# Experts' up projection in three fp32r passes, normalising on ScalarE, shared buffers in a GNN and mixture-of-experts layer

## The chip, the core and the metric

One core of a Trainium2 chip runs the whole layer. The metric is the time of one launch in microseconds of the device; lower is better. The engines that matter here are TensorE (PE for matmuls, PEld for loading the stationary operand), VectorE (DVE), ScalarE (ACT), GpSimd (POOL), and the queue of SyncE (SP), which starts most of the transfers.

## What is computed

The reference is a graph attention layer over 4096 nodes of 512 values, a dense feed-forward net, and then a mixture of experts. The change lies in the last part only:

```python
def _L0_ffn_ref(x, router_w, w1, b1, w2, b2, gamma, beta):   # x: 4096 rows of 512, 8 experts, 256 hidden
    logits = xf @ router_w
    gate_vals, idx = jax.lax.top_k(logits, 2)
    gates = jax.nn.softmax(gate_vals, axis=-1)
    for e in range(E):
        h = jax.nn.relu(xf @ w1[e] + b1[e]) @ w2[e] + b2[e]
        y = _layernorm(xf + h, gamma[e], beta[e])
        w = jnp.sum(jnp.where(idx == e, gates, 0.0), axis=-1)
        out = out + w[:, None] * y
    return out
x = x + _L0_ffn_ref(_layernorm(x, axis=-1)[None], ...)[0]
```

All of it is float32. The kernel computes each row only for the two experts that the router picks.

## The kernel before

The program is a row of blocks with a barrier between them: sorting the edges and the projections of q, k, v, attention, output projection with feed-forward net, and `experts`, which runs alone from about 2945 us to the end. In it every engine has its own instruction stream, and the streams are ordered by semaphores. A `Ring` counts the tiles of a buffer: `ring.wait(eng, i, u)` waits until tile u of turn i is done.

`experts` has four stages.

The router stage takes the 32 tiles of 128 rows of z3 in four turns of eight, each in two halves. PE transposes a tile (L2094), ACT copies it to `z_cols` (L1912), and after four tiles PE multiplies with the router weights (L2107). DVE copies the result (L1969), PE turns it back (L2116), DVE keeps the logits (L1971). SP loads the rows ahead, and behind them, in one queue, b1, w1, w2, b2, gamma, beta and the first rows of x3 (L1794 to L1800).

The list stage is a chain on DVE with some matmuls: top two experts, the place of each row in a list sorted by expert, and which expert each slot of 128 rows has (`expert_of`). It ends with `row_of` (L2042), which sets `s_ready`. Every engine then waits for `s_ready` and for the weights (`s_w`).

The loop takes 72 slots in nine turns of eight (`TURN`). For slot u: POOL gathers the rows by an indirect DMA (L1844) and adds b2 to them (L1852, `res`); PE transposes them (L2094); ACT copies the columns to `zT` (`columns`, L1922); PE multiplies with w1 (`up`, L2150); ACT copies the result (`hidden`, L1927), PE transposes it (L2157), ACT applies bias and Relu (`hidden_columns`, L1934); PE multiplies with w2 (`down`, L2165). DVE adds `res` (L2051, into `y`), takes mean and variance (L2053, L2055), ACT the square root (L1951), DVE the reciprocal (L2057) and normalises (L2058). POOL multiplies by gamma (L1869), DVE adds beta (`shift`, L2064), SP stores the tile.

The order of each engine's stream is written out by hand. PE, in step u: rows of u+2, up of u+1, down of u, hidden of u+1 turned. ACT: `columns(u+2)`, `hidden(u+1)`, `hidden_columns(u+1)`, square root of u. DVE: `norm(u)`, `shift(u-1)`; the last step of a turn has `shift(7)` behind it. POOL: gather of u+4, residual of u+1, gamma of u. `zT`, `up_ps`, `down_ps`, `res` have two buffers, `y` four. `expert(eng, i, u)` reads the number of the slot's expert into a register of the engine, ahead of each operation that uses that expert's weights.

The sum stage gathers for each node its two results (L1897), DVE adds them, times the gates, to x3 (L2080, L2082), and SP stores.

An fp32 matmul stands in the trace as two records of each call.

## Time and profile before

| what | us |
|---|---|
| median of 3 runs | 3532.98 |
| fastest and slowest of them | 3523.99 and 3536.39 |
| the profiled execution's own time | 3529.53 |
| its span, first to last instruction | 3527.8 |
| mean granted TensorE clock | 0.902 of full |

Busy over the whole span: PE 80%, DVE 71%, POOL 62%, PEld 51%, ACT 42%. These are averages over stages with different limits, so the profile has to be read by stage. A timeline line has the start in us, the duration in us, the engine, the line and the operands, and in brackets the idle time of the engine before it and what ended that.

### The profile page before, as it was taken

The numbers are of one execution on the slowest core, as the hardware profiler recorded it, in microseconds if no ns is written. First come the engines' busy times: TensorE is split into PE (matmuls) and PEld (weight loads), VectorE is DVE, ScalarE is ACT, GpSimd is POOL, SyncE is SP. The second block draws the span as 40 slices with busy tenths as digits, with TensorE's granted clock in tenths as the row PEclk, the third lists the DMA queues.
The fourth block names the chain that finished last, engine by engine and source line by source line (L and its number), as shares of the span: only waits on it lengthen the run. The fifth ranks groups of instructions, "written<-read, shape, count | busy, mean of one in ns | idle before, by whom it ended". The sixth has DMA issues, their size and how long they took to land. (4 is left out here: it accounts for less than half of the span.)

```text
span 3527.8 us, 57760 instructions
## 1 busy us (share of the span) xinstructions
PE 2810.0 (80%) x12074; PEld 1806.6 (51%) x12075; DVE 2507.1 (71%) x5087; ACT 1472.7 (42%) x4642; POOL 2197.7 (62%) x2242
## 2 busy tenths in 40 slices
PE   7888888853878888886888888884999997699950
PEld 5555555531333333334665555553888884466630
DVE  6766666634989999999888888885555551577764
ACT  6322222212655655565554544542344442144420
POOL 2477777776777777776777777771222220188866
PEclk9788888876999999998999999996999998799985
DMA  3444444444777777776777777776222223533349
GB/s 104 175 153 157 138 151 159 138 158 124 210 208 210 209 208 206 210 209 187 213 213 213 211 212 213 213 213 212 85 86 86 86 70 119 201 110 113 113 127 314
DMA packets 234986, 594.26 MB, mean 168 GB/s; under 512 B 51889, under 2 KB 60978, under 8 KB 229938
## 3 DMA queue, kind: packets, MB, share of 16 engines
q0 software_dynamic: 127104, 362.93, 36.3%
q1 hardware_dynamic: 103666, 222.27, 17.7%
q10 hardware_dynamic: 4032, 7.34, 0.6%
q14 instruction: 158, 1.29, 0.1%
q8 instruction: 26, 0.43, 0.1%
HBM read 500.22 MB, written 92.15 MB: 168 GB/s over the span
## 5 line engine op out<-in xcount | busy, mean ns | idle before, releaser
L1214 PE MATMUL at_bank<-product,v_hot 128*128 128x260 f32 x2432 | 629.3, 403 | 119.9 <-DVE product L970 110.6
L1168 PE MATMUL at_bank<-wide,hot_t 128*128 x1216 | 611.8, 625 | 127.8 <-ACT hot_t L1036 66.8
L803 POOL DMA_INDIRECT fetched<-t_k,at_index x608 | 583.0, 959 | 192.8 <-issue 134.1
L812 POOL DMA_INDIRECT fetched<-t_v,at_index x608 | 579.1, 953 | 195.2 <-issue 132.3
L348 POOL DMA_INDIRECT records<-staged,address x544 | 533.3, 980 | 265.0 <-issue 164.9
L1214 PEld LDWEIGHTS at_bank<-product,v_hot 128*128 128x128 f32 x2432 | 442.5, 195 | 301.2 <-issue 126.8
L886 DVE TENSOR_TENSOR product<-at_bank,fetched 128x512 f32<-128x512 f32 x608 | 412.6, 680 | 53.0 <-issue 37.1
L970 DVE TENSOR_TENSOR product<-fetched,at_turn 128x520 f32<-128x520 f32 x608 | 404.4, 686 | 61.8 <-DMA fetched<-t_v,at_index 30.1
L1168 PEld LDWEIGHTS at_bank<-wide,hot_t 128*128 128x128 f32 x1216 | 205.4, 193 | 381.7 <-issue 336.1
L617 PE MATMUL qkv_prod<-wide 128*128 128x512 f32 x768 | 378.2, 653 | 0.0
L843 DVE TENSOR_REDUCE raw_score<-product 128x7 f32<-128x448 f32 x608 | 347.1, 573 | 0.0
L1044 ACT ACTIVATE product<-product 128x64 f32<-128x64 f32 x912 | 228.1, 250 | 282.2 <-DVE product L886 281.2
L1109 ACT ACTIVATE v_hot<-at_shared 128x128 f32<-128x128 f32 x608 | 188.1, 309 | 363.2 <-PE at_bank L1214 362.8
L961 DVE TENSOR_TENSOR wide<-at_bank,wide 128x260 f32 x608 | 230.8, 420 | 61.8 <-issue 29.1
L617 PEld LDWEIGHTS qkv_prod<-wide 128*128 128x128 f32 x768 | 158.9, 211 | 193.4 <-issue 193.4
L1396 POOL TENSOR_TENSOR f_base<-f_x 128x512 f32<-128x512 f32 x32 | 41.3, 1291 | 331.0 <-DVE f_x L1445 328.9
L1078 ACT ACTIVATE at_shared<-iota_f,low_neg 128x128 f32<-128x128 f32 x608 | 234.9, 386 | 2.4 <-ACT v_hot L1109 2.1
L598 PE MATMUL ranks<-counts,low_hot_t 128*128 (+1 forms) x1088 | 178.4, 337 | 66.6 <-issue 53.2
L598 PEld LDWEIGHTS ranks<-counts,low_hot_t 128*128 128x128 f32 x1088 | 175.6, 257 | 71.9 <-issue 71.7
L1573 PE MATMUL f_up<-f_zT,f_w 128*128 128x256 f32 x1536 | 189.8, 284 | 0.0
L1573 PE MATMUL f_down<-f_w,f_hT 128*128 128x512 f32 x768 | 185.6, 397 | 2.3 <-issue 2.3
L1573 PEld LDWEIGHTS f_up<-f_zT,f_w 128*128 128x128 f32 x1536 | 185.1, 190 | 2.1 <-ACT f_h L1530 1.3
(294 smaller groups left out, 4253.8 us busy)
## 6 DMA issues: line engine op xcount, KB each, us to landing
row_bc<-in_src SPq DMA_DIRECT2D x34, 1024.0 KB, 4.7
by_slot<-m_y SPq DMA_DIRECT2D x72, 256.0 KB, 2.0
low_bc<-low_row SPq DMA_DIRECT2D x34, 512.0 KB, 5.5
fetched<-t_k,at_index POOLq DMA_INDIRECT x608, 3.7
fetched<-t_v,at_index POOLq DMA_INDIRECT x608, 3.8
records<-staged,address POOLq DMA_INDIRECT x544, 2.1
t_v<-wide SPq DMA_DIRECT2D x32, 260.0 KB
wide<-in_x SPq DMA_DIRECT2D x32, 256.0 KB, 2.9
```

What stands on the lines that cost most here:

```text
L348: eng.indirect_dma_start(records, bass.IndirectOffsetOnAxis(address[:, b, u:u + 1], 0), staged[:, b, u, :], None,).then_inc(put[b][u], 16)
L598: nc.tensor.matmul(ranks[b % 2][:, u * BLOCKS:(u + 1) * BLOCKS], low_hot_t[:, b % 2, u * P:(u + 1) * P], counts[:, :, bass.ds(i * 2 * B + ...
L617: last = nc.tensor.matmul(prod[n][:, :], zT[:, c, kc * P:(kc + 1) * P], w[:, n, kc, :], start=(kc == 0), stop=(kc == KC - 1))
L803: eng.indirect_dma_start(fetched[:, n % SLOTS, 0:C], None, k, bass.IndirectOffsetOnAxis(index[:, t:t + 1], 0)).then_inc(s_row[n % SLOTS], 16)
L812: eng.indirect_dma_start(fetched[:, n % SLOTS, :], None, v, bass.IndirectOffsetOnAxis(index[:, t:t + 1], 0)).then_inc(s_row[n % SLOTS], 16)
L843: nc.vector.tensor_reduce(raw[:, b, u % PAIR, u // PAIR, 0:heads], product[:, u % 4, 0:heads * D].rearrange("p (h d) -> p h d", d=D), AX.X ...
L886: nc.vector.tensor_tensor(product[:, u % 4, 0:C], q_edge[u % 4][:, :], fetched[:, u % SLOTS, 0:C], ALU.mult).then_inc(r_product.sem(u), 1)
L970: nc.vector.tensor_tensor(product[:, u % 4, :].rearrange("p (h w) -> p h w", h=HEADS), fetched[:, u % SLOTS, :].rearrange("p (h w) -> p h ...
L1078: nc.scalar.activation(away[:, u % 4, :], iota_f[:, :], ACT.Abs, bias=low_neg[:, bass.ds(back_of(m) * TURN + u, 1)]).then_inc(r_v_away.sem ...
L1168: nc.tensor.matmul(q_edge[u % 4][:, :], hot_t[:, g % 2, u % BATCH * P:(u % BATCH + 1) * P], q_sb[:, bass.ds(at, 1), :].rearrange("p a c -> ...
L1214: last = nc.tensor.matmul(bank[g % 2 * 2 + n][:, 0:HALF], hot[:, u % 4, :], product[:, u % 4, n * HALF:(n + 1) * HALF], start=first, stop= ...
L1573: last = nc.tensor.matmul(out, stationary(a, k), moving(b, k), start=(k == 0 and n == 0), stop=(k == chunks - 1 and n == len(PASSES) - 1))
```

## The change

1. `up` multiplies in fp32r. w1 and the columns are split into a large part (rounded to fp32r) and a small part (what is left), and three products are summed: large by large, large by small, small by large. Each 128x256 product is one record instead of two, and there are 12 records for a slot instead of 8.
2. The large part of the columns is ACT's copy, the small part a new subtraction on DVE, `small_columns(u+2)`, ahead of `norm(u)`; the first two stand ahead of the loop.
3. w1 is no longer loaded by SP. ACT's queue loads one expert at a time (512 KB) in the router stage, ACT rounds it (`large_w1`, ahead of the second tile of each half), DVE subtracts (ahead of its copy of the router's result).
4. DVE no longer normalises. It computes `offset` = -mean / root (one column), and ACT applies scale and offset in one Identity activation behind the square root.
5. `y`, `res`, `h_sb`, `hT` lie in the memory of `z_cols`; raw w1 and, at the end, `acc` lie in that of two experts' w2; the list stage's one-hot buffers lie in `zT` and `rows_sb`. So SP waits with w2 for the last small part of w1, and loads the first rows of x3 only after the last `down`.

```diff
-        w1_sb, w2_sb = sb("w1", [P, E, KC, F]), sb("w2", [P, E, FC, C])
+        w1_sb = sb("w1", [P, 2, E, KC, F], F32R)
+        w2_sb = sb("w2", [P, E, FC, C])
...
-        zT = sb("zT", [P, 2, C])
-        z_cols = sb("z_cols", [P, 2, KC, HALF * P])
+        zT = sb("zT", [P, 2, 2, C], F32R)
+        early = sb("early", [P, 2 * KC * HALF * P])
...
+        z_cols = early[:, :].rearrange("p (b k r) -> p b k r", b=2, k=KC)
...
+        y, res, h_sb, hT = reused(0, 4, C), reused(4 * C, 2, C), reused(6 * C, 2, F), reused(7 * C, 2, FC, P)
+        acc = w2_sb[:, 0:2, :, :].rearrange("p e f c -> p (e f) c")
+        raw = w2_sb[:, 0:2, :, :].rearrange("p e f c -> p e (f c)")
...
-            eng.dma_start(w1_sb[:, :, :, :], w1.rearrange("e (k p) f -> p e k f", p=P)).then_inc(s_w, 16)
+            r_w1_small.wait(eng, T // TURN - 1, 1)
             eng.dma_start(w2_sb[:, :, :, :], w2.rearrange("e (k p) c -> p e k c", p=P)).then_inc(s_w, 16)
...
             by_turn(eng, TURNS, store)
+            e_down.wait(eng, TURNS - 1, TURN - 1)
+            for u in range(HALF):
+                eng.dma_start(acc[:, u, :], x3[u * P:(u + 1) * P, :]).then_inc(c_x3.sem(u), 16)
...
         @block.scalar
...
+            def load_w1(i, half):
+                r_w1_small.wait(eng, i, half - 2)
+                eng.dma_start(raw[:, half, :].rearrange("p (k f) -> p k f", k=KC),
+                              w1[bass.ds(i * 2 + half, 1), :, :].rearrange("a (k p) f -> p (a k) f", p=P)
+                              ).then_inc(r_w1_raw[half], 16)
+
+            def large_w1(i, half):
+                eng.wait_ge(r_w1_raw[half], i * 16 + 16)
+                nc.scalar.copy(flat(w1_sb[:, 0, bass.ds(i * 2 + half, 1), :, :].rearrange("p a k f -> p a (k f)")),
+                               raw[:, half, :]).then_inc(r_w1_large.sem(half), 1)
+
+            load_w1(0, 0)
+            load_w1(0, 1)
...
+                    if m == 1:
+                        large_w1(i, half)
                     r_turn.wait(eng, i, u)
...
+                    if more and m == HALF - 1:
+                        load_w1(i + 1, half)
...
                     e_var.wait(eng, i, u)
-                    nc.scalar.activation(root[:, :], mean_var[:, 1:2], ACT.Sqrt, bias=eps[:, :]).then_inc(e_root.sem(u), 1)
+                    nc.scalar.activation(spread[:, :], mean_var[:, 1:2], ACT.Sqrt, bias=eps[:, :]).then_inc(e_root.sem(u), 1)
+                    e_offset.wait(eng, i, u)
+                    nc.scalar.activation(y[:, u % 4, :], y[:, u % 4, :], ACT.Identity, bias=offset[:, :], scale=root[:, :]
+                                         ).then_inc(e_norm.sem(u), 1)
...
         @block.vector
...
+                    r_w1_large.wait(eng, i, half)
+                    of = bass.ds(i * 2 + half, 1)
+                    nc.vector.tensor_tensor(flat(w1_sb[:, 1, of, :, :].rearrange("p a k f -> p a (k f)")), raw[:, half, :],
+                                            flat(w1_sb[:, 0, of, :, :].rearrange("p a k f -> p a (k f)")), ALU.subtract
+                                            ).then_inc(r_w1_small.sem(half), 1)
...
                 e_root.wait(eng, i, u)
-                per.link(nc.vector.reciprocal(root[:, :], root[:, :]))
-                nc.vector.tensor_scalar(mine, mine, mean_var[:, 0:1], root[:, :], ALU.subtract, ALU.mult
-                                        ).then_inc(e_norm.sem(u), 1)
+                e_norm.wait(eng, i, u - 1)
+                per.link(nc.vector.reciprocal(root[:, :], spread[:, :]))
+                nc.vector.scalar_tensor_tensor(offset[:, :], mean_var[:, 0:1], -1.0, root[:, :], ALU.mult, ALU.mult
+                                               ).then_inc(e_offset.sem(u), 1)
+
+            def small_columns(i, u):
+                e_zT.wait(eng, i, u)
+                e_up.wait(eng, i, u - 2)
+                nc.vector.tensor_tensor(zT[:, 1, u % 2, :], turned[u % 2][:, :], zT[:, 0, u % 2, :], ALU.subtract
+                                        ).then_inc(e_zT_small.sem(u), 1)
...
+            def body(i, more):
                 for u in range(TURN):
+                    if u < TURN - 2 or more:
+                        small_columns(i, u + 2)
                     norm(i, u)
                     if u:
                         shift(i, u - 1)
                 shift(i, TURN - 1)
...
             def up(i, u, e):
                 e_zT.wait(eng, i, u)
+                e_zT_small.wait(eng, i, u)
                 for kc in range(KC):
-                    last = nc.tensor.matmul(up_ps[u % 2][:, :], zT[:, u % 2, kc * P:(kc + 1) * P], flat(w1_sb[:, e, kc, :]),
-                                            start=(kc == 0), stop=(kc == KC - 1))
+                    for a, b in ((0, 0), (0, 1), (1, 0)):
+                        last = nc.tensor.matmul(up_ps[u % 2][:, :], zT[:, a, u % 2, kc * P:(kc + 1) * P],
+                                                flat(w1_sb[:, b, e, kc, :]), start=(kc == 0 and a == b),
+                                                stop=(kc == KC - 1 and a == 1))
```

## Rows read from the trace of the kernel before

**Rows 1.** Busy time by stretch: stretch, length, each engine's busy (records), clock, DMA, GB/s
```profile
core 0: us, PE busy (x) PEld busy (x) DVE busy (x) ACT busy (x) POOL busy (x), PEclk, DMA share, GB/s
2945.00:3016.00 71.00, 55.24 (x221) 22.95 (x221) 6.77 (x15) 18.77 (x33) 1.45 (x9) 0.86 0.63 202
...
3025.00:3039.00 14.00, 1.92 (x8) 1.78 (x8) 12.52 (x33) 0.00 (x0) 0.00 (x0) 0.50 0.99 416
...
3081.00:3400.00 319.00, 299.15 (x1224) 196.88 (x1223) 244.45 (x408) 135.88 (x354) 261.42 (x220) 1.00 0.34 110
```

**Rows 2.** Timeline: the first and the last residual add of the 72
```profile
3076.00 0.69 DVE L2051 TENSOR_TENSOR m_y<-m_down,m_res 128x512 f32<-128x512 f32 x1 [16.94 <-PE m_down L2165]
...
3409.38 0.68 DVE L2051 TENSOR_TENSOR m_y<-m_down,m_res 128x512 f32<-128x512 f32 x1
```

**Rows 3.** Timeline of one slot: DVE and the square root
```profile
3216.71 0.69 DVE L2051 TENSOR_TENSOR m_y<-m_down,m_res 128x512 f32<-128x512 f32 x1 [0.75 <-PE m_down L2165]
...
3218.50 0.29 ACT L1951 ACTIVATE m_root<-m_mv,m_eps 128x1 f32<-128x1 f32 x1 [0.85 <-DVE m_mv L2055]
...
3219.03 0.81 DVE L2058 TENSOR_SCALAR m_y<-m_y,m_mv,m_root 128x512 f32<-128x512 f32 x1
...
3219.89 0.69 DVE L2064 TENSOR_TENSOR m_y<-m_y,m_beta 128x512 f32<-128x512 f32 x1
```

**Rows 4.** Timeline of another slot: DVE and POOL from normalising to the next add
```profile
3181.65 0.55 DVE L2058 TENSOR_SCALAR m_y<-m_y,m_mv,m_root 128x512 f32<-128x512 f32 x1
...
3182.37 1.27 POOL L1869 TENSOR_TENSOR m_y<-m_y,m_gamma 128x512 f32<-128x512 f32 x1 [0.79 <-DVE m_y L2058]
3182.51 1.67 DVE L2064 TENSOR_TENSOR m_y<-m_y,m_beta 128x512 f32<-128x512 f32 x1 [0.32 <-issue]
...
3184.11 0.68 DVE L2051 TENSOR_TENSOR m_y<-m_down,m_res 128x512 f32<-128x512 f32 x1
```

**Rows 5.** Chain that ended last, ahead of the loop: start us, us, what
```profile
3015.85 22.79 DMA m_beta<-in_L_ffn_beta
```

**Rows 6.** Timeline: the last operation of the list stage
```profile
3058.83 0.23 DVE L2042 CAST m_row_of<-m_down 128x72 int32<-128x72 f32 x1 [2.50 <-PE m_down L2139]
```

**Rows 7.** Groups by line, 3100 to 3400 us: count, busy us, mean ns, idle before
```profile
L2150 PE MATMUL m_up<-m_w,m_zT 128*128 x516 | 127.6, 390 | 11.8 <-issue 10.3
...
L1951 ACT ACT_TABLE_LOAD x7 | 9.0, 1283 | 0.1
```

**Rows 8.** Groups by line in the feed-forward stage, 2500 to 2930 us
```profile
L1573 PE MATMUL f_up<-f_zT,f_w 128*128 128x256 f32 x1392 | 170.4, 282 | 0.0
...
L1409 DVE TENSOR_TENSOR f_zT<-f_turned,f_zT 128x512 fp32r<-128x512 f32 x28 | 18.0, 686 | 38.0 <-ACT f_zT L1538 38.0
```

**Rows 9.** Groups by line, ACT, whole span: a 128x512 activation with constants
```profile
L1036 ACT ACTIVATE hot_t<-hot_t 128x512 f32<-128x512 f32 x152 | 93.2, 613 | 0.0
```

**Rows 10.** Groups by line, 2395 to 2470 us: weights split into large and small
```profile
L1409 DVE TENSOR_TENSOR f_w<-f_raw,f_w 128x1024 fp32r<-128x1024 f32 x4 | 4.9, 1225 | 2.6 <-ACT f_w L1511 2.4
L1508 ACT ACTIVATE f_w<-f_raw,f_gain 128x1024 fp32r<-128x1024 f32 x4 | 4.6, 1153 | 1.2 <-DMA f_raw<-in_L_gnn_W 0.9
...
L1511 ACT CAST f_w<-f_raw 128x1024 fp32r<-128x1024 f32 x4 | 4.2, 1044 | 2.8 <-DMA f_raw<-in_L_gnn_W 2.8
```

**Rows 11.** Timeline of half a turn of the router stage: last copies, router matmuls
```profile
2969.97 1.07 ACT L1912 COPY m_z_cols<-m_turned 128x512 f32<-128x512 f32 x2 [0.26 <-PE m_turned L2094]
...
2971.17 3.59 PE L2107 MATMUL m_down<-m_z_cols,m_router 128*8 128x512 f32 x8 [0.75 <-ACT m_z_cols L1912]
```

**Rows 12.** Timeline: the first sum of the last stage
```profile
3423.66 0.75 DVE L2080 SCALAR_TENSOR_TENSOR m_acc<-m_rows,m_gate,m_acc 128x512 f32<-128x512 f32 x1 [8.85 <-DMA m_rows<-by_slot,m_index]
```

**Rows 13.** Busy time by stretch: of the sort, of attention, of the feed-forward stage
```profile
224.00:251.00 27.00, 22.01 (x110) 14.99 (x110) 15.01 (x43) 5.39 (x8) 20.60 (x22) 0.81 0.49 172
988.00:1067.00 79.00, 63.01 (x188) 25.43 (x188) 71.80 (x137) 46.31 (x221) 60.10 (x63) 0.96 0.72 207
...
2477.00:2954.00 477.00, 464.29 (x2811) 408.23 (x2809) 237.32 (x490) 189.62 (x397) 118.50 (x97) 0.99 0.25 86
```

49 lines of the change are left out of this document (27 added, 22 removed).

## The prediction, written before the change was run

> **What bounds the kernel now.** I first read the busy times by stage [rows 1]. The diff touches only the last block, the mixture of experts: the router stage (2945 to 3016 us), the list stage (to 3058), the loop over the 72 slots, and the weighted sum. In the loop the reader is to see TensorE busy 299 of 319 us, DVE 244, POOL 261 and ACT only 136, at full clock. It looks like a matmul bound, but TensorE is no lone bottleneck. From the first residual add to the last there are 333.4 us for 71 steps [rows 2], 4.70 us a slot, so TensorE works 4.4 and idles 0.3 of each.
>
> Next the timeline of one slot on DVE [rows 3]. From the residual add (L2051, 3216.71) the chain runs through the batch-norm pair to the square root on ACT (3218.50), back to the reciprocal and to the normalising op L2058 (3219.03): 2.32 us. Every step waits for the one before, whatever TensorE does. Then come L2058, L2064 (adding beta to the slot before), and the next add. In the other timeline [rows 4] L2058 takes 0.55, L2064 begins 0.32 after its end, in the same moment in which POOL multiplies by gamma, and takes 1.67 instead of 0.68, and the next add starts at 3184.11. So a slot whose chain DVE carries alone lasts about 2.32 + 0.86 + 1.60 = 4.78 us. That serial path is as long as TensorE's, and the prediction turns on what becomes of it.
>
> For the other stages: the last weight transfer, issued at 3015.85, lands 22.79 later, at 3038.6 [rows 5], while the list is done only at 3058.83 [rows 6]. The weights have 20 us to spare.
>
> **The change part by part.**
>
> *Up projection, TensorE.* Now 1.98 us a slot (127.6 us over 64.5 slots) [rows 7]. The stage before runs the same three-pass form, 128x256, at 170.4 us for 1392 records, 0.122 each [rows 8]; 12 of them are 1.47 us. TensorE gains 0.51 us a slot, down to 3.9. It is worth 36 us only if nothing else holds the slot.
>
> *Small half of the columns, DVE.* One subtraction PSUM minus SBUF, 128x512 to fp32r: 0.686 in the FFN stage [rows 8]. It is put ahead of the residual add and needs the columns that ACT copies.
>
> *Normalising moves to ACT.* DVE drops L2058 (1.085 mean, 0.55 alone) and gets a one-column op, about 0.17 as the reciprocal has in such a chain; ACT gets a 128x512 Identity with scale and bias per partition. Bounds: 0.61 with constants [rows 9]; a per-partition operand adds 1.153 - 1.044 = 0.11 on 1024 columns [rows 10], so two make 0.83. I take 0.8; it can't cost nothing, as it stands between two waits.
>
> *The new DVE path.* Residual add to the offset op: 2.32 as before. What follows is the expert's register load, then L2064. In one slot [rows 4] L2064 starts 0.86 after the start of L2058, while in the other [rows 3] L2058 took longer (0.81) and L2064 followed at once, so the 0.86 counts from the issue of the op before it, and shortening that op doesn't shorten it. Then L2064 0.70, the small columns 0.70, the next add: 2.32 + 0.86 + 0.70 + 0.70 = 4.58 us.
>
> *The new path over ACT.* The columns copy for slot u+2 is behind the Identity of slot u-1 on ACT. Before, it started right behind the 0.29 square root and nobody on DVE wanted it. Now: 2.32, offset op to ACT 0.21, Identity 0.75 (back-to-back ACT ops overlap a little), columns 0.59, hand-over 0.04, small columns 0.70 = 4.61. Two rings of the same length, both above TensorE's 3.9 and POOL's 3.84 (261.4/319 of 4.70). The slot becomes 4.6, not 4.2.
>
> *Port.* L2064 and POOL's gamma collide now. After, L2064 starts 0.86 behind the offset op; gamma can start at 0.21 + 0.8 + 0.18 = 1.19 (0.18 is POOL's delay behind L2058's end [rows 4]). DVE is first, and L2064 stays at 0.70.
>
> *End of each turn of eight.* After slot 7 DVE does beta for slots 6 and 7 before the next small columns; slot 7's has to wait for gamma: 2.32 + 1.19 + 1.50 + 0.05 + 0.70 + 0.70 = 6.46. The table load of ACT at the head of a turn (1.28) [rows 7] ends at 0.21 + 0.8 + 0.17 + 1.28 + 0.59 = 3.05 after the offset op, under the 3.44 of that path, so it is hidden; the second lies in ACT's idle time. Step 0 to 1 has no beta and takes the ACT ring.
>
> *Loop.* 8 x 6.46 + 9 x 4.61 + 52 x 4.6 + 2 x 3.9 (the last two have no small columns) = 51.7 + 41.5 + 239.2 + 7.8 = 340.2 against 333.4: +6.8. Bounds: 4.48 a slot (Identity at 0.61, the DVE path overlapping the register load), 0 to -2; 4.75 (waits not fully hidden), +16.
>
> *Router stage.* ACT rounds one expert's w1 to fp32r (128x1024, 1.044 [rows 10]) ahead of the second columns copy of each half turn, eight times. In the half turn shown the last copies start at 2969.97 and the router matmuls wait for them until 2971.17, 0.75 idle [rows 11]. TensorE's fourth transposition waits for the second copy, and the copies are back to back in pairs, so the cast pushes the second, third and fourth copy back by its length: 8 x 1.04 = +8.3. DVE's subtraction (1.225 [rows 10]) lies under the 3.59 us of matmuls [rows 11]. The eight 512 KB loads are issued behind the fourth copy and have a half turn and more to land; the first two share the start with 2 MB of rows, +1.
>
> *Weights, SP queue.* Loading w2 waits for the last w1 subtraction, because raw w1 lies in w2's space: issue near 3018 instead of 2997, behind it b2, gamma, beta. But 4 MB are gone from the queue; 10 MB at the 416 GB/s seen [rows 1] need 25 us, done near 3045. The list ends near 3068. Hidden, 20 us spare; 0. Moving w1 off the queue gains nothing for the same reason.
>
> *x3 rows.* Loaded only after the last down projection, SP's queue behind the last store. The first sum waits 8.85 us for gathers anyway and starts at 3423.66 [rows 12], some 9 us after the last store is issued; 1 MB lands in less. 0 to +2, I take 0. The shared buffers y, h, hT and the lists have no wait that the order of the stages doesn't already meet.
>
> *Clock.* Here rows speak against the change. With TensorE 97% busy (FFN) the granted clock is 0.99; with 81% busy in the sort stage it is 0.81, with 80% in attention 0.96 [rows 13], and the experts' loop at 94% has 1.00 [rows 1]. The new loop has 3.9/4.75 = 82%. At half clock (1.2 of 2.4 GHz) TensorE needs 7.8 us a slot against 4.6, so each microsecond at half clock costs 0.4. Attention's 0.96 means 8% of the time: 340 x 0.08 x 0.4 = +11; the sort stage's 0.81 means 38%, +52; none is 0. I take a third of attention's share, +4, since no row tells how the chip weighs this mix, and the idle pieces here are spread evenly. The Trainium skill, "TensorE: Matmul & The Clock Gate", section "HAM oscillation", ties a fall to long idle gaps; by it there would be none here and the sum 4 us less. Whether the falls of the other stages came behind such gaps isn't shown by these rows.
>
> *Sum.* 6.8 + 8.3 + 1 + 4 = +20 on the profiled execution's 3529.5 us (span 3527.8): 3549.5. The median, 3533.0, is 3.5 above that execution, and runs scatter by 12 us, so I set 3551.
>
> **The rivals.**
>
> R1, the matmul gain comes through. It would if DVE's register load isn't counted from the issue and ACT takes the Identity in a gap, POOL being less disturbed. 4.70 - 0.51 = 4.19 a slot gives 71 x 4.19 + 8 x 1.8 = 312, -21, with router +9: 3521 (3508 to 3524). For it: DVE and POOL get rid of a contended op; steps as short as 4.1 occur now. Against: the two rings.
>
> R2, the clock falls as in the sort stage: +15 +52 at the worst, half of that likelier: 3575 to 3600.
>
> R3, the port goes to POOL. If the Identity ended before L2064 starts (under 0.47 us, or beta late by 0.3), L2064 would last 1.67 in every slot, as it does in one now [rows 4]: 71 x 0.98 = +70, 3620. That is the point from which it decides.
>
> R4, Identity isn't in the table of the square root: two loads of 1.28 in every slot, 72 x 2.56 = +184, 3735. Copy and Relu, however, run in all eight slots of a turn with one load before the square root (7 loads in 64 slots [rows 7]). The Trainium skill ("ScalarE: Activation LUTs", "Table sets") puts identity with relu and copy in every set; then there is no load, and the sum stays.
>
> R5, the clock holds and the router casts find idle time of ACT: 3551 - 4 - 8 = 3539.
>
> **How the numbers follow.** Forecast (3540 to 3564) 0.55, R5 0.05, R1 0.20, R2 0.12, R3 0.06, R4 0.02. The range 3512 to 3592 leaves out R3, R4, the lowest quarter of R1 and the highest third of R2, about 0.17. The likeliest case's own range is 3540 to 3564. 0.3% is 10.6 us, about what a measurement of this kernel can tell from no change, so the bounds are 3522.4 and 3543.6. Faster: three quarters of R1 and a little of the scatter, 0.17. Same: the rest of R1, R5 and 0.15 of the forecast, 0.25. Slower: the rest, 0.58.
>
> **What would show it.** L2150's group 1.47 us a slot; residual add to residual add 4.6 in the middle of a turn and over 6 at its boundary; TensorE busy about 82% of the loop; beta at 0.68 and no longer 1.67; ACT's Identity 0.75 to 0.83; the router stage 8 to 10 us longer; the time from last weights to list end still positive; granted clock under 1.00 in the loop. Wrong it would be if the step fell under 4.4 (then beta follows the offset op at once, or the columns copy runs ahead of the Identity), or if the loop shows half clock for over 30 us.

## The result, and the profile after

| | before | after |
|---|---|---|
| median, us (runs) | 3533.34 (4) | 3562.77 (4) |
| fastest and slowest | 3523.99 and 3536.39 | 3560.29 and 3563.92 |
| span of the profiled execution | 3527.8 | 3562.2 |
| mean granted TensorE clock | 0.902 | 0.902 |

The ratio is 1.0089, with a 95% interval of 1.0075 to 1.0103: the changed kernel is slower, by 0.9%. The profiled executions of columns_first and act_best_small (below) were among the slower runs of their kernels, so what is read from them rests as well on identity_late and best_three, whose profiles were not. The span grew by 34.4 us. It splits at four operations of the timeline, the counterparts of [rows 2, 6, 12]:

```profile
3067.92 0.23 DVE L2083 CAST m_row_of<-m_down 128x72 int32<-128x72 f32 x1 [2.50 <-PE m_down L2193]
...
3084.71 0.69 DVE L2092 TENSOR_TENSOR m_early<-m_down,m_early 128x512 f32<-128x512 f32 x1 [1.24 <-PE m_down L2222]
...
3442.62 0.68 DVE L2092 TENSOR_TENSOR m_early<-m_down,m_early 128x512 f32<-128x512 f32 x1
...
3457.05 0.75 DVE L2134 SCALAR_TENSOR_TENSOR m_w<-m_rows,m_gate,m_w 128x512 f32<-128x512 f32 x1 [8.70 <-DMA m_rows<-by_slot,m_index]
```

The list is done 9.1 us later than before (3067.92 against 3058.83), of which 2.4 lie ahead of the block. From there to the first residual add it takes 0.4 less than before. The loop, first to last residual add, takes 357.9 us against 333.4: +24.5. Last add to first sum is 14.43 against 14.28, the rest 105.1 against 104.1. So seven tenths of the loss are in the loop.

Busy time by stretch, most of the loop after, to be held against the third row of [rows 1]:

```profile
3085.00:3427.00 342.00, 291.00 (x1480) 186.50 (x1478) 238.94 (x470) 186.87 (x419) 239.37 (x216) 1.00 0.31 101
```

TensorE fell from 94% to 85% busy, VectorE from 77% to 70%, POOL from 82% to 70%, and ScalarE rose to 55%. No engine is near full, yet most slots got longer: the limit is a path, not an engine. The groups by line of the loop, 3090 to 3432 us, name its links (count, then busy us, mean ns of one, and the idle time ahead with what ended it):

```profile
L2206 PE MATMUL m_up<-m_w,m_zT 128*128 x809 | 116.2, 292 | 18.7 <-issue 17.2 <-DVE m_zT L2106 1.4
...
L1864 POOL TENSOR_TENSOR m_early<-m_rows,m_b 128x512 f32<-128x512 f32 x68 | 87.7, 1290 | 1.1
L1881 POOL TENSOR_TENSOR m_early<-m_early,m_gamma 128x512 f32<-128x512 f32 x67 | 85.8, 1280 | 76.6 <-ACT m_early L1986 76.6
...
L1986 ACT ACTIVATE m_early<-m_early,m_offset,m_root 128x512 f32<-128x512 f32 x67 | 54.5, 814 | 56.1 <-DVE m_offset L2100 56.1
...
L2106 DVE TENSOR_TENSOR m_zT<-m_turned,m_zT 128x512 fp32r<-128x512 f32 x67 | 46.3, 692 | 30.0 <-ACT m_zT L1955 29.5 <-issue 0.3
...
L2112 DVE TENSOR_TENSOR m_early<-m_early,m_beta 128x512 f32<-128x512 f32 x67 | 46.3, 691 | 30.4 <-issue 18.9 <-POOL m_early L1881 11.3
...
L2100 DVE SCALAR_TENSOR_TENSOR m_offset<-m_mv,m_root 128x1 f32<-128x1 f32 x67 | 37.4, 558 | 2.6 <-DVE m_root L2099 0.3
```

The up projection fell to 0.144 us a record (116.2 over 809), 1.72 for the twelve of a slot. ScalarE's Identity lasts 0.81. VectorE's offset operation, one column, lasts 0.56 in the mean. POOL, which used to be the busiest helper, now waits 76.6 us for the Identity.

The timeline of one slot and a half shows why (some VectorE, ScalarE and POOL rows from it; the residual add of VectorE is L2092, that of POOL L1864):

```profile
3195.25 1.28 POOL L1881 TENSOR_TENSOR m_early<-m_early,m_gamma 128x512 f32<-128x512 f32 x1 [1.05 <-ACT m_early L1986]
...
3196.67 0.99 POOL L1856 DMA_INDIRECT m_rows<-t_z,m_index  x1
...
3197.67 1.29 POOL L1864 TENSOR_TENSOR m_early<-m_rows,m_b 128x512 f32<-128x512 f32 x1
...
3198.49 0.50 DVE L2100 SCALAR_TENSOR_TENSOR m_offset<-m_mv,m_root 128x1 f32<-128x1 f32 x1
3199.03 0.82 ACT L1986 ACTIVATE m_early<-m_early,m_offset,m_root 128x512 f32<-128x512 f32 x1 [0.77 <-DVE m_offset L2100]
3199.36 0.69 DVE L2112 TENSOR_TENSOR m_early<-m_early,m_beta 128x512 f32<-128x512 f32 x1 [0.36 <-issue]
3199.75 0.56 ACT L1955 CAST m_zT<-m_turned 128x512 fp32r<-128x512 f32 x1
3200.02 1.27 POOL L1881 TENSOR_TENSOR m_early<-m_early,m_gamma 128x512 f32<-128x512 f32 x1 [1.06 <-ACT m_early L1986]
...
3200.34 0.69 DVE L2106 TENSOR_TENSOR m_zT<-m_turned,m_zT 128x512 fp32r<-128x512 f32 x1 [0.30 <-ACT m_zT L1955]
```

Read it along POOL. Its residual add runs from 3197.67 to 3198.96. The offset operation, issued at 3198.49, ends at 3198.99, 0.03 behind the end of POOL's residual add, where 0.16 is its length alone. So it is in all 57 slots in which it lasts over 0.2 us: it ends 0.02 to 0.04 behind that end. Identity follows at 3199.03, gamma at 3200.02 behind it, and then POOL's own queue: gather, and the next residual add. Gamma to gamma is 4.77, and every link is there: residual 1.29, 0.03 to the end of the offset operation, 0.04, Identity 0.82, 0.17, gamma 1.27, 0.15, gather 0.98, 0.02. It is a ring that passes from POOL to VectorE, from there to ScalarE and back to POOL, and TensorE isn't in it.

Twice in a turn POOL copies the next gather indices (L1847). In the middle of a turn it waits 0.91 with the gather behind the copy. The residual add then starts later, and the offset operation waits through all of it:

```profile
3227.74 1.01 POOL L1856 DMA_INDIRECT m_rows<-t_z,m_index  x1 [0.91 <-PE m_turned L2148]
...
3228.67 1.40 DVE L2100 SCALAR_TENSOR_TENSOR m_offset<-m_mv,m_root 128x1 f32<-128x1 f32 x1
3228.76 1.28 POOL L1864 TENSOR_TENSOR m_early<-m_rows,m_b 128x512 f32<-128x512 f32 x1
```

The steps between residual adds in a turn are 6.58 (slot 7 to 0), 4.63, 4.68, 4.77, 4.77, 5.67, 4.78, 4.76: 40.6 us against 37.6 before.

### The profile page after: what moved, and what is told of

Same layout as the page of the kernel before. It is cut to its first block and busy times, and to the rows that moved or that the text cites. A ratio compares the mean times of both kernels' runs of the same rounds, so it can differ in the third digit from the quotient of the medians.

```text
span 3562.2 us, 59000 instructions
## 1 busy us (share of the span) xinstructions
PE 2801.9 (79%) x12362; PEld 1794.8 (50%) x12363; DVE 2510.5 (70%) x5167; ACT 1535.3 (43%) x4722; POOL 2181.2 (61%) x2242
## 5 line engine op out<-in xcount | busy, mean ns | idle before, releaser
L1169 PEld LDWEIGHTS at_bank<-wide,hot_t 128*128 128x128 f32 x1216 | 206.4, 194 | 381.4 <-issue 333.4
L384 ACT ACTIVATE qkv_root<-qkv_mv,qkv_eps 128x1 f32<-128x1 f32 x64 | 18.9, 295 | 395.9 <-DVE qkv_mv L96 395.9
```

Source lines behind the costliest of these rows:

```text
L1169: nc.tensor.matmul(q_edge[u % 4][:, :], hot_t[:, g % 2, u % BATCH * P:(u % BATCH + 1) * P], q_sb[:, bass.ds(at, 1), :].rearrange("p a c -> ...
```

## The experiments

The kernels of group 1 in the table share a chip on which the kernel before took 3533.61 (7 runs). Those of groups 2 and 3 ran on another chip, where the kernel before took 18 to 21% longer (before: 4259.66 and 4163.65), and where the stages ahead of the block, whose code is the same in all, ended anywhere between 3718 and 3826 us (first residual add). Their intervals are up to 1.2% wide to either side, so ratios of those two groups can't decide differences of 1%. I read their loops instead, first to last residual add: their operations have the same durations as on the first chip (offset 0.16 alone, Identity 0.81, residual 1.28, gamma 1.27, gather 0.99), though no profile of the kernel before or of the changed one was taken there, so their loops are held against those of the first chip. The loops also differ in how often TensorE's granted clock fell to half; where that matters it is said.

| kernel | group | loop, us | median, us | ratio to before |
|---|---|---|---|---|
| before | - | 333.4 | 3533.34 | 1 |
| changed | - | 357.9 | 3562.77 | 1.0089 |
| one_pass | 1 | 358.7 | 3564.05 | 1.009 (1.0072 to 1.0108) |
| res_short | 1 | 342.6 | 3548.95 | 1.0048 (1.0031 to 1.0065) |
| cast_late | 1 | 359.2 | 3558.54 | 1.0076 (1.0059 to 1.0093) |
| act_norm | 1 | 355.4 | 3554.0 | 1.0054 (1.0035 to 1.0074) |
| dve_norm | 2 | 344.1 | 4295.57 | 1.0168 (1.0091 to 1.0244) |
| identity_late | 2 | 363.6 | 4292.93 | - |
| loads_early | 2 | 328.2 | 4251.89 | 1.0052 (1.0002 to 1.0103) |
| best_three | 2 | 480.4 | 4426.73 | 1.0461 (1.0376 to 1.0545) |
| columns_first | 3 | 357.7 | 4203.4 | 1.0034 (0.9974 to 1.0094) |
| act_best | 3 | 349.8 | 4222.6 | 1.0103 (0.9987 to 1.0219) |
| act_best_small | 3 | 480.3 | 4315.07 | 1.0385 (1.0326 to 1.0444) |
| dve_cast | 3 | 344.2 | 4232.6 | 1.0191 (1.0132 to 1.0251) |

**one_pass: is TensorE in the path?**

```diff
-                    for a, b in ((0, 0), (0, 1), (1, 0)):
+                    for a, b in ((0, 0),):
```

The kernel leaves out the two products with a small part.

> The changed kernel with one product (large by large) instead of three in the up projection; the two products with a small part are left out, so its output is less exact. All other work stays, the small columns on DVE too. Theory A (the ring DVE, square root, offset op, Identity, columns, small columns sets the slot at 4.77 us, and TensorE waits in it): TensorE loses 8 records, about 0.98 us a slot, and the step from residual add to residual add stays 4.77; the time stays within 5 us of the changed kernel. Rival B (TensorE, or the clock that follows it, still sets the slot): 72 x 0.98 = about 70 us less, or, if the clock falls because TensorE is less busy, longer by 10 us and more.

The loop took 358.7. A turn's steps are 6.80, 4.64, 4.67, 4.76, 4.76, 5.66, 5.20 and 4.43. The expectation named a fall of the clock as the other outcome, and there were falls: the granted clock was 0.91 over the loop, with TensorE 75% busy, and at half during part of two steps in each turn, those of 6.80 and 5.20. The steps at full clock decide: 4.64 to 4.76 and 5.66, within 0.02 of the changed kernel's, with eight of twelve up-projection records gone. In these TensorE isn't in the path. The step of 5.20 and the one of 4.43 behind it together take 0.1 more than the changed kernel's two, the boundary 0.2 more; what they would be at full clock isn't shown.

**res_short: does POOL hold the offset operation?**

```diff
-                eng.tensor_tensor(res[:, u % 2, :], rows_sb[:, u % TURN, :], flat(b2_sb[:, e, :]),
+                eng.tensor_tensor(res[:, u % 2, 0:1], rows_sb[:, u % TURN, 0:1], flat(b2_sb[:, e, 0:1]),
```

POOL adds one column; the other 511 of the residual are left out.

> The changed kernel with POOL's residual add (rows plus b2) cut from 512 columns to one; the other 511 columns of the residual are left out. Theory A1 (the offset op on DVE, 0.16 alone, waits up to 0.35, and once a turn 1.25 us, until POOL's residual add lets go of a path to SBUF that both use): the offset op takes 0.16 in every slot, the step falls from 4.77 to 4.4 to 4.5 and the one of 5.67 disappears; a turn goes from 40.65 to about 38.5, the loop is 18 to 20 us shorter. Rival A2 (the op itself costs 0.5 in this place, whatever POOL does): nothing changes in the loop, under 3 us. Rival C (POOL's own chain of gather, residual and gamma sets the slot): it loses 1.3 us a slot and the loop 50 us or more.

Loop 342.6, -15.3, where 18 to 20 were expected. Offset operation and what follows in one slot:

```profile
3196.31 0.68 DVE L2092 TENSOR_TENSOR m_early<-m_down,m_early 128x512 f32<-128x512 f32 x1
...
3198.61 0.16 DVE L2100 SCALAR_TENSOR_TENSOR m_offset<-m_mv,m_root 128x1 f32<-128x1 f32 x1
3198.81 0.81 ACT L1986 ACTIVATE m_early<-m_early,m_offset,m_root 128x512 f32<-128x512 f32 x1 [0.43 <-DVE m_offset L2100]
3199.47 0.69 DVE L2112 TENSOR_TENSOR m_early<-m_early,m_beta 128x512 f32<-128x512 f32 x1 [0.70 <-issue]
```

It lasts 0.16 in all 72 slots, and 42 of the 71 steps are 4.42 to 4.44. 4.42 is the ring over ScalarE that the prediction had at 4.61: 2.30 to the offset operation, 0.20, then, start to start, 0.72 (Identity), 0.59 (columns), 0.61 (small columns). The step with the index copy stayed at 5.3, which I had expected to fall further, and three of the boundary steps, with half clock in them, took 7.1 to 7.2 instead of 6.5. A reservation: a short residual add also takes 1.1 us out of POOL's ring, so this run alone doesn't separate holding the offset operation from POOL's queue being long. In the timeline they are one ring.

**cast_late: what do the casts cost in the router stage?**

```diff
-                    if m == 1:
-                        large_w1(i, half)
...
-                    if more and m == HALF - 1:
-                        load_w1(i + 1, half)
+                    if m == HALF - 1:
+                        large_w1(i, half)
+                        if more:
+                            load_w1(i + 1, half)
```

> The changed kernel with ACT's rounding of w1 behind the fourth columns copy of each half turn instead of ahead of the second, so that it runs beside the router matmuls. If the cast in the copies' path costs what was forecast (1.04 us, eight times), the router stage is 8 us shorter and nothing else moves. Rival: the weights, now rounded and loaded later, delay the next rounding or w2, and the stage or the start of the loop is as late as before or later; then 0 or positive.

The first residual add came at 3077.67 instead of 3084.71, 7.0 us earlier. Of these 1.2 lie ahead of the block, where the kernels don't differ; from the block's start to the end of the list cast_late takes 5.9 less, so the casts cost 5.9 here and not 8.3. The same move gives 6.5 between columns_first and act_best and 7.4 between dve_norm and dve_cast. The loop was 1.3 longer, with two clock falls (6.10 and 6.03 between adds) instead of one.

**act_norm: only the normalising moved, in the kernel before.**

```diff
-                    nc.scalar.activation(root[:, :], mean_var[:, 1:2], ACT.Sqrt, bias=eps[:, :]).then_inc(e_root.sem(u), 1)
+                    nc.scalar.activation(spread[:, :], mean_var[:, 1:2], ACT.Sqrt, bias=eps[:, :]).then_inc(e_root.sem(u), 1)
+                    e_offset.wait(eng, i, u)
+                    nc.scalar.activation(y[:, u % 4, :], y[:, u % 4, :], ACT.Identity, bias=offset[:, :], scale=root[:, :]
+                                         ).then_inc(e_norm.sem(u), 1)
```

> The kernel before with the second half of the change alone: offset op on DVE, scaling by Identity on ACT; up projection in fp32, w1 loaded by SP, no shared buffers, no small columns. Theory A: without small columns no DVE op waits for ACT's columns copy, the DVE path is 2.31 + 0.5 + 0.4 + 0.7 = 3.9 us a slot and TensorE's 4.15 to 4.4 sets it; the loop goes from 333 to 305 to 320 us, the time is 15 to 25 us under the kernel before. Rival D (normalising on ACT is itself the loss: Identity's 0.81 stands in the way of ACT's copies for TensorE): the step is 4.7 or more and the time the same as before or longer.

VectorE's part of the edit is as in the change. Loop 355.4, +22.0 over the kernel before, where 305 to 320 us were expected: this part alone costs nearly what the whole change costs in the loop. The same wait is in its timeline, between POOL's residual add and the Identity:

```profile
3208.09 1.27 POOL L1853 TENSOR_TENSOR m_res<-m_rows,m_b 128x512 f32<-128x512 f32 x1
...
3208.36 1.03 DVE L2063 SCALAR_TENSOR_TENSOR m_offset<-m_mv,m_root 128x1 f32<-128x1 f32 x1
...
3209.42 0.81 ACT L1954 ACTIVATE m_y<-m_y,m_offset,m_root 128x512 f32<-128x512 f32 x1 [1.29 <-DVE m_offset L2063]
```

The offset operation lasts 0.80 in the mean of 72 slots. POOL's residual adds follow each other at 4.73 to 4.77 in most of a turn, the changed kernel's step again, with fp32 matmuls in place of the three passes. VectorE's adds are less even, 4.42 to 5.05 in a turn's middle, and wait up to 1 us and more for the down projection: fp32 matmuls of 1.99 a slot stand in a second ring (Identity, columns, up two slots on, down, add), so it isn't shown that all of the 22 is POOL's.

**dve_norm and dve_cast: three passes, normalising back on VectorE.**

```diff
-                nc.vector.scalar_tensor_tensor(offset[:, :], mean_var[:, 0:1], -1.0, root[:, :], ALU.mult, ALU.mult
-                                               ).then_inc(e_offset.sem(u), 1)
...
+                nc.vector.tensor_scalar(mine, mine, mean_var[:, 0:1], root[:, :], ALU.subtract, ALU.mult
+                                        ).then_inc(e_norm.sem(u), 1)
```

ScalarE's Identity goes with it. dve_cast has the edit of cast_late as well.

> The changed kernel with normalising back on DVE (L2058 of the kernel before), three-pass up projection, small columns, router casts and shared buffers kept. Theory E (the ring through ACT's in-order stream is the price of the new normalising, but DVE couldn't have carried both): DVE has 2.31 + 0.87 + 1.6 + 0.61 = 5.4 us a slot where beta meets gamma, 4.6 where it doesn't; the loop is 340 to 375 us. At the lower end it is faster than the changed kernel's 358, and moving the normalising was itself the loss; at the upper end the three passes would be worse without it. Rival F (small columns cost nothing, DVE has room): the loop falls to 300 to 320.

> The changed kernel with the normalising back on VectorE (one tensor_scalar, ScalarE only the square root) and the rounding of w1 behind the fourth columns copy; three passes, small columns and shared buffers stay. Nothing is left out. If moving the normalising to ScalarE was itself the loss in the loop, the loop falls from 358 to 344 (as three passes with normalising on VectorE gave on a chip whose earlier stages were slower), and with 7 less in the router stage the whole stands at 3562.8 - 14 - 7 = 3542, still above the kernel before, as the small columns take 0.69 of VectorE in every slot. If the normalising's place doesn't matter, the loop stays at 358 and the whole at 3556. If three passes were a gain by themselves, loop below 333 and whole below 3530.

The loops took 344.1 and 344.2, 14 less than the changed kernel's and 11 more than that of the kernel before. The step in the middle of a turn is 4.48, and its ring is again POOL's:

```profile
3944.35 1.29 POOL L1864 TENSOR_TENSOR m_early<-m_rows,m_b 128x512 f32<-128x512 f32 x1
...
3944.89 1.05 DVE L2096 TENSOR_SCALAR m_early<-m_early,m_mv,m_root 128x512 f32<-128x512 f32 x1
...
3946.12 1.56 POOL L1881 TENSOR_TENSOR m_early<-m_early,m_gamma 128x512 f32<-128x512 f32 x1 [0.47 <-DVE m_early L2096]
...
3947.82 0.99 POOL L1856 DMA_INDIRECT m_rows<-t_z,m_index  x1
...
3948.83 1.28 POOL L1864 TENSOR_TENSOR m_early<-m_rows,m_b 128x512 f32<-128x512 f32 x1
```

Residual 1.29, 0.30 to the end of the normalising, 0.18, gamma 1.56, 0.14, gather 0.99, 0.02: 4.48. The held normalising ends 0.28 to 0.31 behind POOL's operation in all 53 slots of dve_norm in which it is held, whether it lasts 0.74 or 1.96, and gamma can start. With the normalising on ScalarE it is 0.03 + 0.04 + 0.82 + 0.17 until gamma starts, against 0.30 + 0.18, so 0.58 more; gamma gets 0.29 back, as no beta runs beside it. The difference is the 0.29 us of a step. The totals of both, 1.7% and 1.9% over the kernel before, don't fit the loops' 11 us (0.3%), and the expected 3542 can't be held against them; I don't use them. In both, stretches of four or five slots run at 5.36, where beta meets gamma and lasts 1.55 or more. There are two in each kernel, and each begins in a step with half clock (0.68 in the mean), the only such steps of the loop: a fall seems to tip this order of work into the slower one for some slots, which no run here tests.

**identity_late: columns and hidden copies ahead of the Identity.** The columns copy of slot u+3 and the hidden copy of slot u+2 stand between square root and Identity of slot u.

```diff
+                    if u < TURN - 3 or (more and u < TURN - 1):
+                        columns(i, u + 3)
+                    if u < TURN - 2 or (more and u < TURN - 1):
+                        hidden(i, u + 2)
                     e_offset.wait(eng, i, u)
```

> The changed kernel with ACT's order altered: the columns copy of u+3 and the copy of hidden u+2 go ahead of the Identity of u, behind the square root. Theory G (the columns copy that stands behind the Identity closes the ring at 4.77): DVE no longer waits for columns, its own path 2.31 + 0.87 + 0.70 + 0.61 = 4.5 sets the slot, whatever the offset op waits for POOL; a turn falls from 40.65 to about 38, the loop by 20 to 24 us. Rival H (only the blocked offset op counts, wherever the copy stands): the same 4.77, under 3 us.

**columns_first: the columns copy alone.** As identity_late, without `hidden(i, u + 2)`, which stays where it was.

> The changed kernel with one move: ScalarE copies the columns of slot u+3 between the square root and the Identity of slot u, instead of slot u+2's behind the Identity of slot u-1. Nothing is left out. Ring theory: the 4.77 us step of the changed kernel is the way offset op, Identity, columns copy, small columns, residual add; with the copy ahead of the Identity that way is gone, what is left is VectorE's own path of 2.30 + 0.87 + 0.69 + 0.69 = 4.55, and the loop falls from 358 to some 343 us (4.4 a slot if POOL's residual add leaves the offset op alone after the shift, 335). Rival: VectorE's own path is the limit already and the offset op's wait for POOL is all there is: steps stay at 4.75, loop 356 to 360. Second rival: the copy now stands in the way of the Identity and takes the place of the old wait, as the hidden copy did when both were moved: 5.0 and more, loop above 360.

The loops took 363.6 and 357.7: taking the copy off the way gained nothing. If the ring over ScalarE, in the form the prediction gave it, set the slot, these two would have been 15 to 24 us shorter, as was expected of them; it doesn't set it. The steps are 4.38 where the offset operation is free, which is VectorE's own path, and 4.76 where POOL holds it, to the hundredth the changed kernel's. Two steps in each turn got worse (6.81 and 7.2 instead of 5.67 and 6.58). In identity_late the granted clock fell to half eight times, in columns_first once. A turn with a fall takes some 0.8 more (steps of 5.3 to 5.4 for 4.4, partly made up behind it), so most of the 6 us between the two loops is that, by this estimate. The first of the worse steps in the timeline of columns_first:

```profile
3850.72 3.13 DVE L2114 TENSOR_TENSOR m_early<-m_early,m_beta 128x512 f32<-128x512 f32 x1 [0.70 <-issue]
...
3850.80 1.28 POOL L1864 TENSOR_TENSOR m_early<-m_rows,m_b 128x512 f32<-128x512 f32 x1
...
3852.02 1.27 POOL L1881 TENSOR_TENSOR m_early<-m_early,m_gamma 128x512 f32<-128x512 f32 x1
```

Beta, 0.69 alone, begins with POOL's residual add, and ends 0.56 behind the gamma that follows it without a gap. In the changed kernel the offset operation is the one held there, and beta comes after the residual add. Here the offset operation got through in 0.16, and beta, 0.70 behind its end, is the first to meet POOL. The same step in identity_late takes 6.81 too.

**loads_early: the register loads moved ahead, in the kernel before.** VectorE reads the expert's number while it waits for the square root, TensorE one slot ahead.

```diff
                 nc.vector.bn_aggr(mean_var[:, :], stats[:, :]).then_inc(e_var.sem(u), 1)
+                e = expert(eng, i, u - 1) if u else None
                 e_root.wait(eng, i, u)
```

> The kernel before, nothing of the change, with two register loads of the expert's number moved: on DVE ahead of the wait for the square root, on TensorE behind the down projection's issue. If the 0.86 us from the issue of L2058 to the start of L2064 is that load, beta starts right behind the normalising, ahead of POOL's gamma, takes 0.68 and no longer 1.67, and the DVE path falls from 4.78 to about 3.7; TensorE's up follows the transposition at 0.45 and not at 0.94; the slot is then TensorE's 4.15: the loop goes from 333 to 300 to 310 us, the time down by 23 to 33. Rival: the gaps are something else (loop branch, POOL's port): within 5 us of the kernel before.

Loop 328.2, 5 under that of the kernel before on the first chip, where 300 to 310 were expected. Beta does follow the normalising at once, but its place was taken by POOL's:

```profile
3858.73 1.28 POOL L1852 TENSOR_TENSOR m_res<-m_rows,m_b 128x512 f32<-128x512 f32 x1
...
3858.87 1.43 DVE L2059 TENSOR_SCALAR m_y<-m_y,m_mv,m_root 128x512 f32<-128x512 f32 x1
...
3860.22 0.68 DVE L2065 TENSOR_TENSOR m_y<-m_y,m_beta 128x512 f32<-128x512 f32 x1
```

The normalising lasts 1.43. In the middle of a turn POOL's residual adds follow each other at 4.46 to 4.47, its ring with the normalising on VectorE; VectorE's own steps are uneven, from 2.78 to 6.5.

**act_best: changed kernel, columns_first, register load early on VectorE, casts late.** The edits are those shown above.

> columns_first, and besides VectorE's expert register load put in the wait for the square root, and the rounding of w1 on ScalarE put behind the fourth columns copy of a half turn. Nothing is left out. Theory that three serial costs make the loss (ring over ScalarE, register load behind the offset op, casts in the router stage): the step falls to 2.30 + 0.50 + 0.69 + 0.69 = 4.2 us, the boundary stays at 6.4, so the loop is 8 x 6.4 + 63 x 4.2 = 316, the router stage is 7 shorter, and the whole stands at 3562.8 - 42 - 7 = 3514, ratio to the kernel before 0.995. Rival: POOL, which is busy 3.84 us of each slot and shares a port, takes over: beta starts earlier and meets the gain or the residual add in every slot and lasts 1.6, so 4.9 to 5.1 a slot, loop 355 to 365, and the whole stands at 3555 to 3560.

Loop 349.8, 8 under the changed kernel's, not the 316 expected. Two steps in the middle of a turn are at 4.75 to 4.77 again, although neither the columns copy nor the register load is in the way any more. Two rounds of POOL's ring:

```profile
3885.99 1.28 POOL L1864 TENSOR_TENSOR m_early<-m_rows,m_b 128x512 f32<-128x512 f32 x1
...
3887.33 0.81 ACT L1988 ACTIVATE m_early<-m_early,m_offset,m_root 128x512 f32<-128x512 f32 x1 [0.99 <-DVE m_offset L2103]
...
3888.32 1.27 POOL L1881 TENSOR_TENSOR m_early<-m_early,m_gamma 128x512 f32<-128x512 f32 x1 [1.05 <-ACT m_early L1988]
...
3889.74 0.99 POOL L1856 DMA_INDIRECT m_rows<-t_z,m_index  x1
...
3890.75 1.28 POOL L1864 TENSOR_TENSOR m_early<-m_rows,m_b 128x512 f32<-128x512 f32 x1
...
3891.01 1.05 DVE L2103 SCALAR_TENSOR_TENSOR m_offset<-m_mv,m_root 128x1 f32<-128x1 f32 x1
```

Residual to residual 4.76. This is the plainest sight of the ring: VectorE comes earlier than in the changed kernel and only waits longer, 1.05 instead of 0.50.

**best_three and act_best_small: the small columns in the wait for the square root.** act_best_small is act_best with this edit. best_three has the edits of act_best and this one, and besides the offset computed on ScalarE, the hidden copy early and TensorE's register load early.

```diff
                 nc.vector.bn_aggr(mean_var[:, :], stats[:, :]).then_inc(e_var.sem(u), 1)
+                if u < TURN - 2 or more:
+                    small_columns(i, u + 2)
                 e_root.wait(eng, i, u)
```

> The changed kernel with all of it: w1's cast behind the fourth copy, small columns ahead of the wait for the root, expert loads early on DVE and TensorE, offset computed on ACT (so that no one-column op of DVE meets POOL), columns and hidden copies ahead of the Identity. If the rings are as found, no ring but TensorE's 3.9 to 4.1 and POOL's 3.9 to 4.1 is left: a loop of 300 to 315 us, a time of 3500 to 3518, under the kernel before. If another ring closes (ACT now has 3.4 us of work a slot in a fixed order; the gathers need 12.3 us over three slots), the loop stays above 330.

> act_best, and besides the small columns of slot u+2 put in the wait for the square root instead of ahead of the residual add. Nothing is left out. If VectorE's serial path is the limit, 0.58 us of waiting are filled and the step falls by 0.4 to 0.6 against act_best, down to TensorE's 3.9 and POOL's 3.84: loop 300 to 310, whole 3500 to 3508. If POOL is the limit, nothing falls, or the 0.69 us subtraction meets POOL's residual add and holds the reciprocal back by up to 1.3: steps at or above those of act_best, loop 330 or more.

The loops took 480.4 and 480.3, with steps of 6.15 to 6.25 and of 7.6 to 7.9. The shorter ones are my mistake of order: TensorE's stream has up of u+2 ahead of down of u+1, and the small columns of u+2 now came only behind the residual add of u, so TensorE waits for them, 2.08 us in this slot of act_best_small:

```profile
3921.21 0.69 DVE L2112 TENSOR_TENSOR m_zT<-m_turned,m_zT 128x512 fp32r<-128x512 f32 x1
...
3922.15 1.71 PE L2209 MATMUL m_up<-m_w,m_zT 128*128 x12 [2.08 <-DVE m_zT L2112]
```

The longer ones are the clock's: all of them have half clock in them (0.77 to 0.79 in the mean), 28 and 29 of the 71 steps. The granted clock was 0.90 over both loops, with TensorE 69% busy. There the up projection takes 2.56 instead of 1.71, as in this row of best_three:

```profile
3929.27 2.56 PE L2214 MATMUL m_up<-m_w,m_zT 128*128 x12 [1.13 <-DVE m_zT L2117]
```

At 1.5 us a step that is some 42 of the 122 us that these loops are longer than the changed kernel's (an estimate).

In act_best_small POOL waits for the Identity and the offset operation lasts 0.16 in the mean: with slots of over 6 us the ring of POOL isn't tight.

By the ratios no kernel came out ahead of the kernel before; loads_early has the shorter loop and no shorter time that these runs can tell.

## Why the prediction was right, and where it wasn't

The time, 3562.8, is 12 over the forecast of 3551 and 1.2 inside the upper end of its own range of 3540 to 3564, and the sign is right. That it lies inside is partly luck. Loop and clock together were forecast at 10.8 and came to 24.5, over the loop's own upper bound of 16; the router stage came out 2.6 under its term; the rest, put at nothing, made 3.1, of which 2.4 lie ahead of the block. The direction came from the right thought, that a serial path and not TensorE's work sets the slot; the two paths it named weren't the one that did.

*Up projection, 1.47 a slot.* It became 1.72 (first to last record of twelve), so the gain was 0.26, not 0.51. As foreseen, TensorE doesn't set the slot (one_pass), and this error cost nothing.

*New path over ScalarE, 4.61.* Measured 4.42 where nothing disturbs it (res_short): Identity 0.81 for 0.8, columns and small columns 0.59 and 0.61 start to start for 0.63 and 0.70. Right in its links, 0.2 too long, and 0.35 under the step that was measured: it isn't the limit.

*VectorE's path, 4.58.* Measured 4.38 (columns_first, identity_late). That beta's start counts from the issue of the operation ahead held: 0.87 from the start of a 0.50 us offset operation, 0.86 from that of a 0.16 us one.

*The offset operation, about 0.17.* This is the step that failed. It lasts 0.16 alone, but 0.50 in the middle of a turn and 1.40 behind the index copy. The part "Port" asked only whether beta meets gamma, and that it answered rightly: beta stayed at 0.69. It didn't ask whether the new operation meets POOL's residual add, which is the other operation of POOL. The row to see it by was on the page: in [rows 3] the normalising lasts 0.81 and in [rows 4] 0.55, and I took the longer one as it was, without asking what held it. In the trace before, POOL's residual add stands beside the longer one, and the normalising ends 0.30 behind it:

```profile
3218.25 1.29 POOL L1852 TENSOR_TENSOR m_res<-m_rows,m_b 128x512 f32<-128x512 f32 x1
```

*POOL as 3.84 us of busy time.* The same mistake from the other side. A share of busy time below the step says that POOL isn't full, not that no ring goes through it. Residual, offset, Identity, gamma, gather, residual add up to 1.28 + 0.03 + 0.04 + 0.81 + 0.18 + 1.27 + 0.15 + 0.99 + 0.02 = 4.77, the measured step. POOL's terms could be read before the change; the Identity's 0.81 was estimated at 0.8, and only the hand-overs of 0.03 and 0.04 around the offset operation come from the trace after.

*Loop, +6.8.* Measured +24.5. A turn was to take 38.7 and took 40.6: the step with the index copy is 1.07 over, the other five and that from slot 0 to 1 some 0.8 together, the boundary (6.58 for 6.46) 0.1. Over the eight turns up to the last boundary that is 15.6. The turn with the clock fall adds 1.2 and the first turn 1.0; the last seven steps took 30.8, as forecast. The upper bound of a slot, 4.75, was right for the middle but didn't foresee the 5.67.

*Router stage and start, +9.3.* Measured 6.7 in the two stages; 2.4 more came ahead of them, where the change touches nothing. cast_late gives the casts 5.9 of the 8.3.

*Clock, +4.* One fall in the loop, between two adds 6.06 us apart; that turn took 41.8 instead of 40.6. TensorE was 85% busy, and the granted clock is 1.00 over the loop. The other loops say more than this one. With TensorE 89% busy there was no stretch of half clock (act_norm), at 88% three (res_short), at 85 to 86% one or two, at 84% eight (identity_late), at 75% eighteen (one_pass), at 69% twenty-eight and twenty-nine (best_three, act_best_small). So the busy share, by which I had argued from [rows 13], goes with the falls roughly. The longest idle piece of TensorE grows along with it: 1.2 us in the changed kernel, 2.1 in one_pass, 2.4 in best_three. The Trainium skill, "TensorE: Matmul & The Clock Gate", section "HAM oscillation", ties falls to long idle gaps. For the changed kernel it came closer than my third of attention's share, but these runs don't tell share from gap, and in none of them did a fall need an idle piece of over 2.4 us.

*Weights, SP queue, x3, table loads.* The last weights were issued at 3026.64 and took 23.4 to land, at 3050.0, 18 us ahead of the list (20 forecast). Last add to first sum grew by 0.15. Seven plus seven table loads in 3090 to 3432, two a turn, and none between square root and Identity. All as stated, but that w2 was issued at 3021.8 and not near 3018.

*The rivals.* R1 (the matmul gain comes through) fell by one_pass. R2 and R5 were about the clock: it held but for one fall, nearly as in R5, but the casts didn't hide. R3 (beta behind gamma) was the right place, the port, with the wrong operation, and at a price of 70 us where the whole loop grew by 24.5; columns_first shows that its kind of step does come up, beta at 3.13 behind POOL's residual add and gamma. R4 (table loads) didn't come.

What stays open: how the 24.5 of the loop divide. Moving the normalising alone cost 22.0 (act_norm), and moving it back gained 13.8 (dve_norm, other chip); three passes and small columns with the normalising on VectorE cost 10.7, and that loop has stretches at 5.36. Nor is it shown how much of act_norm's 22.0 is its second ring. The parts don't add up, since each is a step of whichever ring is longest. What sets the speed of the second chip's earlier stages wasn't looked into.

## What to carry to other kernels

Before an operation is moved to an idle engine, list the rings of the steady state, each engine's whole stream among them and not only its busy share, and sum each with the operation in its new place: here a helper at 82% busy became the limit because its next operation came to depend on a 0.8 us one that had not been there. Ask of each new small operation which operand path it shares with a neighbour; a one-column operation can cost as much as the 1.3 us operation that holds it. And where two rows of the same operation differ in length (0.55 and 0.81), find out why before taking either. Look at the granted clock of a loop before its time is read as the price of an edit: a third of what best_three lost in the loop was the clock.

## What the runs showed of the hardware

A VectorE operation with two operands in SBUF waits while POOL's 128x512 tensor operation runs, at one column as at 512: the one-column offset operation took 0.16 with POOL's residual add at one column, and 0.50, 1.05 and 1.40 beside one of 512. In five kernels (the changed one, act_norm, identity_late, columns_first, act_best) all 246 offset operations of over 0.2 us end 0.01 to 0.04 behind the end of that residual add. The normalising, one 128x512 operand and two of one column, took 0.55 alone and up to 1.96 (dve_norm), and ends 0.28 to 0.31 behind POOL's operation. The reciprocal at 3198.29, one operand, took 0.16 in the midst of the same residual add, and the small columns at 3200.34, one operand in PSUM, 0.69 in the midst of gamma. The Trainium skill, "SBUF — State Buffer", section "SBUF: two separate sides", describes this as a lock that the operation starting first keeps for the whole instruction. The wait agrees. That the first to start keeps it doesn't, by the starts that the profile records: the offset operation is recorded 0.09 ahead of POOL's residual add (3228.67 and 3228.76) and ended behind it, and beta is recorded as starting 0.08 ahead of POOL's residual add (3850.72 and 3850.80) and yet ended behind that one and the gamma after it.

The waits run the other way too: POOL's gamma took 1.27 alone and 1.56 where VectorE's beta had started ahead of it (dve_norm, 3946.12).

Reading the expert's number into a register just ahead of beta puts beta's start 0.86 to 0.87 behind the start of the one-column operation before it, whether that lasts 0.16 or 0.50. With the read moved into the wait for the square root, beta starts 0.12 behind the start of a 0.16 us offset operation (act_best_small, 3922.24 and 3922.36).
